# Weights in fourths, ones-matmuls in TensorE's gaps, and 32 items' upper parts on ScalarE, in a cross-attention block

## The reference

```python
q, kv = ln(queries), ln(tokens)                    # each with its own gain and bias
qp, kp, vp = q @ Wq.T + bq, kv @ Wk.T + bk, kv @ Wv.T + bv
scores = qh @ kh.T / sqrt(32) - spatial_scale[h] * dist(query_xy, token_xy) + spatial_offset[h]
scores = where(key_padding, -inf, scores)
x = queries + softmax(scores) @ vh @ Wo.T + bo
h = gelu(ln(x) @ W1.T + b1)                        # W1: 512 to 2048
out = x + h @ W2.T + b2
```

## Time and profile before

| | |
|---|---|
| median of 3 runs | 1252.64 us |
| profiled execution, its own time | 1252.53 us |
| its span, first to last instruction | 1250.7 us |
| busy: TensorE, VectorE, GpSimd, ScalarE | 97%, 78%, 80%, 68% |
| first scores (item 0) | 38.98 us |
| first down projection | about 208 us |

### The profile page before, as it was taken

How to read it: one execution, slowest core, us unless ns; L and a number is a source line. 1 busy time by engine, 2 the same in 40 slices (tenths; PEclk the granted TensorE clock), 3 DMA queues, 4 the chain that set the end, 5 groups by cost and what they waited for, 6 DMA issues and landing times.

```text
span 1250.7 us, 27639 instructions
## 1 busy us (share of the span) xinstructions
PE 1208.7 (97%) x9383; PEld 814.1 (65%) x9383; DVE 978.2 (78%) x2654; ACT 849.6 (68%) x1902; POOL 995.3 (80%) x1285
## 2 busy tenths in 40 slices
PE   5888889999999999999999999999999999999998
PEld 5655456666667666666667676666666666666665
DVE  5699998888878788888878788888888787768311
ACT  5768758676777677676777677776767677766331
POOL 5478888989898898989898998989898997768320
PEclk9889999999999999999999999999999999999999
DMA  6689999888989898989899898989989897878534
GB/s 197 179 186 218 217 204 216 187 200 204 210 193 217 185 215 201 190 197 198 206 202 221 177 219 191 203 199 198 203 206 208 184 213 179 168 175 174 151 108 128
DMA packets 468588, 241.66 MB, mean 193 GB/s; under 512 B 383952, under 2 KB 408800, under 8 KB 468448
## 3 DMA queue, kind: packets, MB, share of 16 engines
q1 hardware_dynamic: 468448, 239.91, 84.7%
HBM read 109.66 MB, written 12.58 MB: 98 GB/s over the span
## 4 chain that ended last, share of the span: by engine, by line
PE 85%; DVE 8%; issue 2%; SPq 1%; ACT 1%; DMA 1%; POOL 1%; POOLq 0%; DVEq 0%; ACTq 0%
PE ps_down L621 26%; PE ps_up L606 26%; PE ps_qk L542 12%; PE ps_vo L566 6%; PE ps_vo L563 5%; PE ps_s L577 4%; PE ps_pv L591 4%; DVE p_nat L1022 2%; DVE soft L1005 1%; DVE w L950 1%; SPq L362 1%; PE ps_down L498 1%; DVE stats L968 1%; DVE x_nat L982 0%; DVE qk_parts L996 0%
## 5 line engine op out<-in xcount | busy, mean ns | idle before, releaser
L606 PE MATMUL ps_up<-hT,w 128*128 128x256 f16 x3072 | 377.2, 273 | 3.0 <-ACT u L762 1.5
L1200 POOL TENSOR_SCALAR p_nat<-soft,row_inv 128x256 f16<-128x256 f32 x512 | 329.9, 654 | 59.1 <-DVE row_inv L1016 58.0
L621 PE MATMUL ps_down<-w,hid 128*128 128x512 f16 x1536 | 372.9, 379 | 0.4 <-DVE hid L1054 0.4
L606 PEld LDWEIGHTS ps_up<-hT,w 128*128 128x128 f16 x3072 | 300.2, 98 | 93.1 <-issue 3.2
L1005 DVE CUSTOM_DVE_ANT_0 soft<-ps_s,soft,factor 128x256 f32<-128x256 f32 x512 | 225.6, 476 | 132.7 <-PE ps_s L577 132.0
L730 ACT ACTIVATE soft<-soft,neg_max 128x256 f32<-128x256 f32 x512 | 255.2, 500 | 108.4 <-DVE neg_max L1005 107.0
L1022 DVE SCALAR_TENSOR_TENSOR p_nat<-soft,row_inv,p_nat 128x256 f16<-128x256 f32 x512 | 291.5, 608 | 1.0 <-POOL p_nat L1200 0.8
L1208 POOL TENSOR_SCALAR soft<-dist,scale_neg,offset 128x512 f32<-128x512 f32 x256 | 248.5, 971 | 12.8 <-DVE p_nat L1022 12.6
L621 PEld LDWEIGHTS ps_down<-w,hid 128*128 128x128 f16 x1536 | 148.7, 97 | 131.9 <-DVE hid L1054 0.9
L762 ACT ACTIVATE u<-ps_up,bias,up_scale 128x256 f32<-128x256 f32 x256 | 142.3, 556 | 131.7 <-PE ps_up L606 130.7
L1216 POOL TENSOR_SCALAR hid<-u,hid_scale 128x1024 f16<-128x1024 f32 x64 | 80.9, 1264 | 104.4 <-ACT u L768 101.2
(11 more groups left out here) (114 smaller groups left out, 1539.1 us busy)
## 6 DMA issues: line engine op xcount, KB each, us to landing
w<-x_scratch SPq DMA_DIRECT2D x256, 256.0 KB, 3.1
stack<-qk_parts SPq DMA_DIRECT2D x256, 96.0 KB
raw<-in_ctx SPq DMA_DIRECT2D x32, 256.0 KB, 3.7
raw<-in_x SPq DMA_DIRECT2D x32, 256.0 KB, 3.1
c_stage<-in_w SPq DMA_DIRECT2D x32, 256.0 KB, 4.0
x<-in_x SPq DMA_DIRECT2D x32, 256.0 KB, 3.4
out<-x SPq DMA_DIRECT2D x32, 256.0 KB, 3.2
tok_rows<-in_tok_xy SPq DMA_DIRECT2D x16, 256.0 KB, 4.5
```

Of the source, the lines that this page charges most:

```text
L606: mm = e.matmul(ps_up[s % 2][:, 0:L], w_1_sb[:, wp, k, m * P:(m + 1) * P], hT[:, b % 2, :, xp * KT + k, :], start=(k, wp, xp) == (0, 0, 0) ...
L621: mm = e.matmul(ps_down[tt][:], hid[:, chunk % HID_RING, i, hp, tt * P:(tt + 1) * P], w_2_sb[:, s % W2_RING, wp, :], start=(m == 0 and (hp ...
L1200: mine = e.tensor_scalar(p_nat[:, nat, HI, lc, :], soft[:, ring, lc, :], row_inv[:, ring, lc:lc + 1], 1.0, ALU.mult, ALU.mult)
```

## The change

- The key and query weights come in fourths (`load_quarters`, 256 KB each, a semaphore each); squares are taken per fourth (`quarter_squares`, into `w_ssq`), and VectorE adds the four. The bias matmuls run over fourths. The first batch's tiles 0 and 1 are loaded before the key weight, tiles 2 and 3 between the two weights.
- TensorE multiplies a tile of ones by itself (`warm`, 128x512 into the bank of `ps_pv`) 10, 3, 10, 8, 2 and 8 times in slots -32, -30, -8, -6, -3 and -2; `keep_busy` starts at slot 0 instead of 7. GpSimd fills that tile.
- For items 0 to 31, GpSimd multiplies `soft` by the reciprocal and the scale in place (`p_normalise`, f32), ScalarE copies it to f16 (`p_hi_first`, one operation of 128x512), and VectorE makes the lower part with one subtraction of 128x512 instead of two fused operations of 128x256; the scaled copy of the reciprocal falls away. Items from 32 on are as before.
- Steps stand elsewhere: in slots 1 to 30 ScalarE does `qk_hi` after the exponentials, VectorE does `qk_lo`, then `p_lo`, then `attn_lo` last; three of four `attn_lo` come one slot later; the sums and norms of the feed-forward weights move within their slots; the setup steps of slots -32 to -1 move (tile steps earlier, the value weight's square from -19 to -6, its load from -26 to -25, `dist_square` from -19 and -18 to -22).

```diff
-                    load_weight(SEC_K)
-                for sec, at_slot in ((SEC_Q, -29), (SEC_V, -26), (SEC_O, -14)):
+                for sec, at_slot in ((SEC_K, -31), (SEC_Q, -29)):
+                    if slot == at_slot:
+                        load_quarters(sec)
+                for sec, at_slot in ((SEC_V, -25), (SEC_O, -14)):
...
-                for b, n in at_tile(slot, (-33, -32, -21, -20), (-31, -30, -28, -28), (-2, -1, 2, 3), (6, 7, 11, 12)):
+                for b, n in at_tile(slot, (-33, -32, -21, -20), (-32, -32, -30, -30), (-2, -1, 2, 3), (6, 7, 11, 12)):
                     load_tile(b, n)
...
+            def warm(count):
+                gate.wait_ge(s_id, ID_FILL)
+                for _ in range(count):
+                    e.matmul(ps_pv[:], fill[:, 0, 0:P], fill, start=True, stop=True)
...
+                for at_slot, count in ((-32, 10), (-30, 3), (-8, 10), (-6, 8), (-3, 2), (-2, 8)):
+                    if slot == at_slot:
+                        warm(count)
...
-                if 7 <= slot < DOWN:
+                if 0 <= slot < DOWN:
...
+            def quarter_squares(sec):
+                for k in range(KT):
+                    gate.wait_ge((s_wk if sec == SEC_K else s_wq)[k], DMA)
+                    gate.wait_ge(s_wsq, KT * AT[sec] - KT + k + 1)
+                    e.activation(square_out[:, k * D:(k + 1) * D], w_stage[sec][:, k, :], ACT.Square,
+                                 accum_out=w_ssq[:, AT[sec], k:k + 1]).then_inc(s_wsq)
...
+            def p_hi_first(i):
+                nat, ring = i % NAT_RING, i % SOFT_RING
+                gate.wait_ge(s_pnorm, i + 1)
+                if i >= NAT_RING:
+                    gate.wait_ge(s_pt[(i - NAT_RING) % PT_RING], n_pt(i - NAT_RING))
+                e.activation(p_nat[:, nat, HI, :, :], soft[:, ring, :, :], ACT.Copy).then_inc(s_phi_first)
...
-                gate.wait_ge(s_phi, i + 1)
+                if i < FIRST:
+                    gate.wait_ge(s_phi_first, i + 1)
+                    e.tensor_tensor(p_nat[:, nat, LO, :, :], soft[:, ring, :, :], p_nat[:, nat, HI, :, :], ALU.subtract).then_inc(s_plo)
+                    return
+                gate.wait_ge(s_phi, i - FIRST + 1)
...
+            def p_normalise(i):
+                ring = i % SOFT_RING
+                gate.wait_ge(s_one, i // 2 + 1)
+                for lc in range(LC):
+                    mine = e.tensor_scalar(soft[:, ring, lc, :], soft[:, ring, lc, :], row_one[:, ring, lc:lc + 1], P_SCALE, ALU.mult, ALU.mult)
+                mine.then_inc(s_pnorm)
...
+                if 1 <= slot < UP:
+                    for which in range(2):
+                        for G in due(slot, QK_PROJ + 2 * which + 1, GROUP, N_HG):
+                            qk_lo(G, which)
+                for i in due(slot, 3, ITEM, FIRST):
+                    p_lo(i)
+                for G in range((UP - 11) // GROUP + 1):
+                    if slot == GROUP * G + (10 if G % HG == HG - 1 else 11):
                         attn_lo(G)
```

More of the change, by code:

```diff
@@ L488, in tensor_program, with weight_bias, value_bias @@
             e, gate = engine, Gate(engine)
-            def weight_bias(sec, m):
-                gate.wait_ge(s_w[sec], DMA)
+            def weight_bias(sec, quarters):
                 gate.wait_ge(s_cols, DMA)
-                if sec == SEC_V:
-                    gate.wait_ge(s_bcol, BIAS_Q)
                 b_ln = B_Q if sec == SEC_Q else B_KV
+                for k in quarters:
+                    gate.wait_ge((s_wk if sec == SEC_K else s_wq)[k], DMA)
+                    for m in range(KT):
+                        col = sec * KT + m
+                        mm = e.matmul(ps_bias[sec][:, col:col + 1], w_stage[sec][:, k, m * P:(m + 1) * P],
+                                      cols_sb[:, b_ln + k:b_ln + k + 1], start=((k, m) == (0, 0)), stop=((k, m) == (KT - 1, KT - 1)))
+                if KT - 1 in quarters:
+                    mm.then_inc(s_brow)
+            def value_bias(m):
+                sec, b_ln = SEC_V, B_KV
+                gate.wait_ge(s_w[0], DMA)
+                gate.wait_ge(s_cols, DMA)
+                gate.wait_ge(s_bcol, BIAS_Q)
                 col = sec * KT + m
@@ L772, in scalar_program @@
                     columns_square()
-                for which in range(2):
-                    for G in due(slot, QK_PROJ + 2 * which + 1, GROUP, N_HG):
-                        qk_hi(G, which)
+                if slot < 1 or slot >= UP:
+                    for which in range(2):
+                        for G in due(slot, QK_PROJ + 2 * which + 1, GROUP, N_HG):
+                            qk_hi(G, which)
                 for G in due(slot, 10, GROUP, N_HG):
@@ L1253, in gpsimd_program @@
                     bias_tile(i)
-                for i in due(slot, 2, ITEM, N_ITEMS):
-                    p_hi(i)
+                for i in due(slot, 2, ITEM, FIRST):
+                    p_normalise(i)
+                for i in due(slot, 2 + FIRST, ITEM, N_ITEMS - FIRST):
+                    p_hi(FIRST + i)
                 for w in range(AT_W1, N_W):
```

152 lines of the change are left out of this document (93 added, 59 removed).

## The result

The changed kernel took 1256.97 us (median of 7 runs, 1255.14 to 1259.82) against 1252.64 (7 runs, 1250.86 to 1253.87): ratio 1.0038 [1.0029, 1.0048], slower by 0.4%. The forecast was 1236.5 in 1226 to 1247: wrong in size and in sign. Its profiled execution took 1256.35 us, the one of before 1252.53.

A forecast was written before the change was run, and what follows sets the result against it. Only work before the first down projection at 208.1 us could move, with VectorE setting the pace from 45.0 to 163.5 us; the last 1042.6 us stay. −6.7 −3.5 −4.8 −1.0 = −16.0 us gives 1236.5, range 1226 to 1247.

The forecast's parts named there:

- Term 1: Start, up to the first exponential: from 45.1 to 38.4 us, −6.7 us, bounds −10 and −3.5.
- Queries: Start, query projection: tile 3 normalised about 17.6, projection at 23.6 instead of 30.60, done 25.0 us.
- bound of −3.5 us: Start, smallest gain: lower clock, 4 matmul groups × 1.35 less gain, and the key weight's path 2 us later still.
- key limb: Start, key weight's path through sums, norm and lower parts: ends about 18.1 instead of 16.05, later by 2 us.
- Term 2: Slots 0 to 8: less VectorE work, 0.48 us a slot, gives −3.5 us, bounds −1 and −6.
- Term 3: Slots 9 to 28: VectorE relieved, paces 3.97 then 3.85 us a slot, −4.8 us, bounds −9 and −1.
- the last rival: Slots: longer hand-over VectorE, GpSimd, ScalarE, VectorE closes a ring; decides at 0.33 us a slot; 1261 us, chance 0.08.
- the second rival: Slots 1 to 31: ScalarE sets the pace, over 4.2 us a slot; 1244 us, chance 0.17.
- the fourth: Slots 29 to 36, chain through DMA queue and ScalarE before the first down projection: −1 us, bounds +3 and −4.
- the last two rivals: Start not earlier, about 1251.5 us, chance 0.05; slots slowed by a longer hand-over, 1261 us, chance 0.08.

The follow-up runs named there:

- start alone: Changed kernel with the old way of making p and the old order within the slots, keeping only the new start: 1253.73 us, 1.0003.
- new p alone: Kernel before with only the new way of making p for 32 items, every step where it was: 1252.06 us, 0.9999.
- after again: The changed kernel run once more, unedited, for a second trace: 1258.05 us, 1.0045 against the kernel before.
- more fill: Changed kernel with TensorE's slots 9 to 21 filled up to 18 steps of 512 columns instead of 16: 1256.15 us, 1.0030.
- 64 halved: Changed kernel with 64 fill matmuls of slots 6 to 30 each cut into two of 256 columns: 1258.97 us, 1.0046.

## Why the prediction was wrong

**Term 1, the start: −2.7 instead of −6.7 us** (−0.1 in the second profile). The step that failed is *Queries*: "tile 3 normalised about 17.6 ... Projection at 23.6". It started at 28.71 (key projection: 23.48, forecast 18.1). TensorE after:

```profile
1.52 4.45 PE L657 MATMUL ps_pv<-attnT 128*128 128x512 f16 x10 [1.52 <-POOL attnT L1331]
...
10.35 6.96 PE L514 MATMUL ps_down<-cols,w_stage 128*128 128x1 f32 x32
17.18 0.57 PE L556 MATMUL ps_up<-sums,one 128*128 128x2 f32 x2
...
19.31 4.33 PE L657 MATMUL ps_pv<-attnT 128*128 128x512 f16 x10
23.48 1.48 PE L570 MATMUL ps_qk<-xT,w_k 128*128 128x256 f16 x12
24.79 1.89 PE L657 MATMUL ps_pv<-attnT 128*128 128x512 f16 x8
28.71 1.47 PE L570 MATMUL ps_qk<-xT,w_q 128*128 128x256 f16 x12 [2.03 <-DVE qk_parts L1069]
```

I had not costed 32 of the bias matmuls at all (8 of the key weight, 24 of the query weight): 6.96 us, ahead of the query weight's total. Its norm then reaches GpSimd, and tile 3 stands behind it there. The chain after:

```profile
18.66 0.98 POOL norm L1236
19.64 1.57 POOL shift L1252
...
21.32 0.78 POOL raw L1254
22.10 0.08 issue
22.18 0.62 POOL x_nat L1271
```

GpSimd does the norm's root at 18.66 and has tile 3 normalised and split at 22.8, where the forecast had it normalised at 17.6. VectorE stood idle for the total too (2.02 us), with the lower part of tile 2 behind it, so both transposes that the query projection needs came late: issued at 21.19 and 24.61 us, the second landed at 28.30, and the projection began at 28.71. Moving the 32 matmuls of the query weight confirms the cause (total 3.1 us earlier, projection 2.1, scores 0.9), and a part of its worth goes back to the clock. It is a part of the miss: 2.1 of the 5.1 us by which the query projection came late. Where the other 3.0 went no run shows.

The ten ones had been put at 4.3 us, and took 4.45 and 4.33; the fall of a projection from 2.72 to 1.4 us was right too. What I took for settled was the level: eight ones at the upper one took 1.89 us (0.24 each), ten before them 0.43 each. The clock, which had risen at 6.4 us, fell at 9.8, after 24 one-column matmuls and three ones with hardly a pause, and rose again at 23.4. The Trainium skill (TensorE: Matmul & The Clock Gate, Part 1) makes the slow state the default, which activity lifts. The trace agrees in that the first ten ones ran at the lower level; between 6.4 and 9.8 us, though, TensorE was hardly idle, nearly all of it with one-column matmuls, and the clock fell all the same.

The bound of −3.5 us doesn't follow from what was named for it: four groups at 1.35 us each are 5.4, which leaves −1.3 of the −6.7 even with no key limb later still.

**Term 2, slots 0 to 8: +1.2 instead of −3.5 us.** VectorE fell from 32.97 to 28.48 us, by more than the 2.8 forecast, but it was no longer what the items waited for. With the new order of steps, eight profiles (this kernel's two and six of the edited ones) reach item 9 between 78.4 and 80.6 us, whether the first exponential came at 42.2 or at 45.1. With the old order and both the new start and new p, three reach it at 74.4 to 75.8, from 41.4 to 42.3; the start alone keeps its lead of 1.8 us too (78.72 against 80.85). So the lead of the start is lost by item 9 in the new order, and it isn't in the old one. Within these slots the chain holds the out-bias matmuls of TensorE, 5.07 us at 61.21 after, 5.35 before; which single step of the new order costs it I have not tried.

**Term 3, slots 9 to 28: +3.8 instead of −4.8 us, the largest miss.** The step that failed is "ScalarE is next: pace 3.97 ... Pace 3.85". The costs were right: the subtraction 681 ns (0.69 undisturbed), the copy 617 ns, VectorE 45.0/13 = 3.46 us a slot (3.6).

Three groups of 80.9 to 134.9 us, after:

```profile
L1098 DVE TENSOR_TENSOR p_nat<-soft,p_nat 128x512 f16<-128x512 f32 x13 | 8.8, 681 | 0.2 <-ACT p_nat L791 0.2
L791 ACT ACTIVATE p_nat<-soft 128x512 f16<-128x512 f32 x13 | 8.0, 617 | 0.1
L1304 POOL TENSOR_SCALAR soft<-dist,scale_neg,offset 128x512 f32<-128x512 f32 x12 | 10.3, 856 | 9.2 <-DVE p_nat L1098 9.2
```

The third row holds the answer: GpSimd stood idle for 9.2 us in front of bias tiles, for the lower part of p. Before, the same wait was 1.4 us. This is the mechanism of the last rival, to which I gave 0.08. The waits from 80 to 165 us, after (us in total, times, longest):

```profile
POOL soft L1304 <- DVE p_nat L1098: 11.9, 8, 2.7
PE ps_s L605 <- DVE neg_max L1078: 11.4, 8, 2.9
```

and with the lower part in its old place:

```profile
...
PE ps_s L605 <- DVE neg_max L1078: 13.1, 13, 1.9
DVE p_nat L1098 <- ACT p_nat L791: 6.5, 6, 1.4
...
POOL soft L1302 <- DVE p_nat L1098: 1.8, 3, 0.8
```

One turn of the ring, in the timeline after (rows between these left out):

```profile
141.98 0.69 DVE L1064 TENSOR_TENSOR v_parts<-ps_vo,v_parts 128x512 f16<-128x512 f32 x1 [3.27 <-ACT v_parts L767]
...
143.64 0.68 DVE L1098 TENSOR_TENSOR p_nat<-soft,p_nat 128x512 f16<-128x512 f32 x1
144.43 0.77 POOL L1304 TENSOR_SCALAR soft<-dist,scale_neg,offset 128x512 f32<-128x512 f32 x1 [2.70 <-DVE p_nat L1098]
145.09 0.51 ACT L783 ACTIVATE soft<-soft,neg_max 128x256 f32<-128x256 f32 x1 [1.41 <-DVE neg_max L1078]
145.60 0.38 PE L605 MATMUL ps_s<-stack 97*128 97x256 f16 x2 [2.91 <-DVE neg_max L1078]
```

ScalarE does the value parts behind its exponentials; VectorE waits 3.27 us for them, and the lower part of p stands last behind it. GpSimd waits 2.70 for that, and TensorE and ScalarE wait for VectorE. GpSimd, busy 26.35 of the 31.36 us of items 22 to 29, does not make it up: it leads the chain of those items, where before VectorE did. The chain's shares by line in these items, after (the view cuts such lines off):

```profile
by line: POOL soft L1287 23.9%; POOL soft L1304 19.1%; issue 14.2%; POOL rstd L1248 6.3%; POOL x L1319 5.3%; POOL x_n L1263 4.9%; POOL x_nat L1271 4.4%; POOL shift L1252 3.9%; POOL raw L1254 2.4%; DVE w L1029 2.4%; ACT soft L783 2.2%; POOL 
```

With the lower part in its old place GpSimd leads too, but its waits are shorter:

```profile
by line: POOL soft L1285 27.8%; POOL soft L1302 20.9%; issue 7.0%; POOL shift L1250 4.4%; SPq L400 4.2%; POOL x L1317 4.2%; POOL h_nat L1274 4.0%; POOL raw L1252 4.0%; POOL norm L1234 3.6%; POOL rstd L1246 3.2%; POOL x_n L1261 2.6%; DVE w L
```

With the new p alone it doesn't: the largest shares are SyncE's, 13.7% for issues of the transposes of p (L373), 12.5% for copies to `stack` (L364), and 11.7% for their landing.

The column of items 22 to 29 is the cleanest evidence: 31.3 to 31.4 us in all six profiles with the lower part last, 28.8 to 29.2 in all five with the new p and the lower part in its old place. That is 2.2 us in seven items, 0.32 a slot, at the point from which the rival was said to decide. The clock isn't behind it: the second profile of after, the one without ones and the one without fill up to slot 21 have no time at the lower level in these items, and take 31.3 to 31.4 us as well. Nor is it lost evenly: in these seven items GpSimd waits for the lower part once, in the turn shown.

But even in the old order term 3 was too large. With the new p alone VectorE is busy 25.89 of 29.06 us in items 22 to 29, and the pace is nearly that of before (29.40): GpSimd (26.18) and SyncE's queue are next. From item 9 to 29 it gains 1.9 us, not 4.8. I had divided the busy time of the next engine by the slots and added 0.07 to 0.15; GpSimd's waits for others, 0.4 us a slot here, did not go away when VectorE got room.

**The clock, from item 9 to 16.** The length of these items goes with the time at the lower level: 28.2 to 30.8 us with up to 10.2 us of it, 32.2 to 34.9 with 13.2 and more. The kernel without fill is the exception that shows how. Three kernels, items 9 to 16 (after, after again, no fill):

```profile
79.37:109.73 30.36, 25.37 (x187) 17.53 (x188) 26.42 (x75) 26.75 (x70) 21.92 (x33) 0.83 0.88 189
```

```profile
79.66:114.54 34.88, 28.61 (x187) 18.97 (x188) 28.01 (x80) 29.08 (x75) 23.90 (x37) 0.72 0.84 188
```

```profile
80.58:110.40 29.82, 23.59 (x160) 19.30 (x161) 25.59 (x73) 25.72 (x66) 21.16 (x32) 0.56 0.86 185
```

At a clock of 0.56 these items are no longer than at 0.83, when no fill stands in front of the real matmuls; with fill and 0.72 they are 4.5 us longer than with fill and 0.83. But the kernel without fill pays in the next items: 27.3 us from 16 to 22, so 57.1 from 9 to 22, between after (55.9) and after again (58.2). This fits two costs, fill at the lower level and the slower real matmuls; they are not told apart, and it isn't shown either which way it goes: longer waits could make the clock fall as well as the other way round. That more fill holds the clock up was my expectation, and it missed: 17.1 us low with more fill, 10.2 and 19.2 in the two profiles of after. What makes the clock fall in one execution and not in another of the same kernel (10.2 and 19.2 us low) stays open.

**The last stretch: +2.4 us.** The step that failed is "I carry 1042.6 us over unchanged". No matmul is added or moved in it, yet TensorE stops once for 1.71 us:

```profile
525.61 1.46 PE L649 MATMUL ps_down<-w,hid 128*128 128x512 f16 x6
528.77 1.47 PE L634 MATMUL ps_up<-hT,w 128*128 128x256 f16 x12 [1.71 <-issue]
```

Its operand is a transpose issued at 522.64, and it landed 6.0 us later. The DMA queues of 523 to 530 us after:

```profile
q14 instruction: 2, 0.02, 1.9%
q8 instruction: 1, 0.02, 0.8%
...
hT<-h_nat SPq DMA_TRANSPOSE x1, 6.0
```

The same around that transpose before:

```profile
q14 instruction: 1, 0.01, 0.2%
...
hT<-h_nat SPq DMA_TRANSPOSE x1, 3.5
```

So three fetches of instructions fall on the slow transpose, one on the quick one. The stop stands 317 to 320 us after the first down projection in eight profiles: 1.50 to 1.73 us in four (after, after again, lower part in old place, start and p in the old order), 0.73 without fill, 0.17 to 0.55 in three (start alone, more fill, 64 halved). Without the ones it is gone there, and three smaller ones (0.34 to 0.52 us) stand 387, 527 and 667 us after the first down projection. The profile with 64 halved matmuls has it at 0.55 and a last stretch 1.5 us shorter. The traces of all fourteen profiles bear the link out. In their last stretches stand 420 transposes of `hT`. The 240 with no fetch of instructions between issue and landing took 3.0 to 3.5 us (median 3.2); with one the median is 3.8, with two 4.4, and the only four with three took 5.8 to 6.0: they are the ones in front of the four long stops. TensorE's idle time in the last stretch is 0.45 us before and 2.38 after, and the stretch less that idle time is 1042.2 to 1042.6 us in all fourteen. So the stops make 1.9 of the 2.4 us, and a transpose that landed late, with three fetches beside it, makes the long one. What puts three fetches there is argued, not shown: it fits fetches that fall elsewhere when instructions are added or taken out ahead, but no run moved the fetches alone, the time of the kernel with 64 halved did not fall (1258.97), and each profile is one execution.

**Rivals and bounds.** ScalarE's pace, the second rival, did not decide: it was busy 48.98 of 54.00 us, but the longest wait was GpSimd's for the lower part of p. The chance of the ring, 0.08, was far too low: the text named its place and the point from which it decides, 0.33 us a slot, and then set the chance by nothing in the trace. It was also taken for a full loss or none; here 0.32 us a slot over some slots, a start worth 2.7 instead of 6.7 and the last stretch gave +4.3 together. The second rival's own sum was wrong too: 3.9 and 15.4/23 make 4.57 a slot, 0.4 more than before, a loss of some 8 us over 20 slots and not a term that vanishes. Three of the four terms had been bounded on the side of a gain alone, at −10 to −3.5, −6 to −1 and −9 to −1 (the fourth at −4 to +3), and the range left the last two rivals out; bounds of terms 2 and 3 above zero would have needed the question what VectorE's waits become, which I asked of ScalarE alone.

## What to carry to other kernels

In a kernel whose engines pass each item around in a ring, ask what each engine would wait for once the full one is relieved (it led the next one by only 8 to 15% here), and cost the position of a step by who waits for it, not by its length: the same 0.7 us step in another place was worth 3 us. An early lead is worth only what the next shared row of work, here the weights of the feed-forward part, leaves of it. Fill matmuls in the queue are a loan: at the lower clock one took 0.43 us instead of 0.24, in front of real ones. And before a stretch is carried over unchanged, ask what else in it depends on the number of instructions ahead: here 1.9 us of stops came with none of its matmuls changed.

## What the runs showed of the hardware

- The granted clock at the start is not the same in two executions of one kernel: a projection of twelve 256-column matmuls took 1.47 us in one and 2.58 in the other at the same place. The time to landing of the same transfer differs as well: 5.75 and 7.41 us into the span for the key weight's first fourth. Together that is 2.7 us of first scores, 1.1 and 1.6.
- 24 one-column matmuls and three of 512 columns, with hardly a pause, did not keep the clock up: it fell at 9.8 us, and the 32 one-column matmuls behind took 6.96 us.
- The clock column of a stretch says 1.00 until the first change of level is on record (48.7 us before), although the projections in it took 2.72 us, the duration of the lower level.
- Transposes of the same form took 3.0 to 3.5 us to land in the steady part with no fetch of instructions beside them, and 5.8 to 6.0 with three; the fetches are packets of up to 16 KB on DMA queues of their own.
